# A sixth of the histogram's column masks moved from VectorE to ScalarE, and another order of the zeroing transfers among the weight loads

## The reference

```python
def _rgcn(x, edge_index, edge_type, weight, root, bias):
    src, dst = (edge_index[0], edge_index[1])
    msgs = x[src]
    out = x @ root + bias
    for r in range(weight.shape[0]):
        mask = (edge_type == r).astype(x.dtype)
        sums = jax.ops.segment_sum(msgs * mask[:, None], dst, num_segments=n)
        cnt = jax.ops.segment_sum(mask, dst, num_segments=n)
        mean = sums / jnp.maximum(cnt, 1.0)[:, None]
        out = out + mean @ weight[r]
    return out
```

## Time and profile before

| | |
|---|---|
| time, median of 3 runs | 1833.63 us (1831.04 to 1833.66) |
| the profiled execution's own time | 1833.66 us |
| its span, first to last instruction | 1832.0 us |
| PE busy | 1740.2 us, 95% |
| DVE busy | 996.4 us, 54% |
| ACT busy | 446.2 us, 24% |
| POOL busy | 712.9 us, 39% |
| mean granted clock of PE | 0.98 |
| queue q1 (SP's): share of 16 DMA engines | 23.5% |

### The profile page before, as it was taken

How to read it: one execution, slowest core, us unless ns; L and a number is a source line. 1 busy time by engine, 2 the same in 40 slices (tenths; PEclk the granted TensorE clock), 3 DMA queues, 4 the chain that set the end, 5 groups by cost and what they waited for, 6 DMA issues and landing times.

```text
span 1832.0 us, 27421 instructions
## 1 busy us (share of the span) xinstructions
PE 1740.2 (95%) x9548; PEld 1438.0 (78%) x9548; DVE 996.4 (54%) x2518; ACT 446.2 (24%) x848; POOL 712.9 (39%) x613
## 2 busy tenths in 40 slices
PE   5998999999999999999999999846999999999999
PEld 4775699978787777778787877634999888879987
DVE  6997999982625354443526286877612234351311
ACT  3327767730101011010101154433000000111100
POOL 2100010036363544536453554000785551446862
PEclk9999999999999999999999999957999999999999
DMA  4435432233231312122233532110454350113322
GB/s 131 132 121 162 127 109 94 88 120 95 61 91 36 95 35 85 46 74 61 65 85 121 175 115 85 29 47 7 130 179 140 104 157 26 47 46 127 89 73 68
DMA packets 132122, 168.42 MB, mean 92 GB/s; under 512 B 14383, under 2 KB 75963, under 8 KB 131767
## 3 DMA queue, kind: packets, MB, share of 16 engines
q1 hardware_dynamic: 104213, 128.21, 23.5%
q10 hardware_dynamic: 21730, 22.51, 3.8%
q0 software_dynamic: 6080, 16.40, 2.9%
HBM read 135.51 MB, written 25.30 MB: 88 GB/s over the span
## 4 chain that ended last, share of the span: by engine, by line
PE 80%; DVE 11%; DMA 3%; DVEq 2%; ACT 2%; issue 2%; POOL 1%; SPq 1%; ACTq 0%
PE ps L363 21%; PE ps L364 21%; PE ps L365 20%; PE ps L1383 9%; DMA w_stage<-in_stream 2%; PE ps L988 1%; DVE w_lo L314 1%; PE ps L1348 1%; DVE adj L974 1%; DVE key_start L868 1%; POOL w_lo L272 1%; PE ps L1303 1%; PE ps L922 1%; SPq L1038 1%; DMA nat<-in_x 1%
## 5 line engine op out<-in xcount | busy, mean ns | idle before, releaser
L363 PE MATMUL ps<-w_hi,xt_hi 128*125 128x512 f32 x1320 | 539.0, 408 | 12.6 <-DVE xt_lo L2260 3.5
L252 POOL TENSOR_TENSOR w_hi<-w_stage,zero 128x512 fp32r<-128x512 f32 x258 | 279.4, 1083 | 679.6 <-PE ps L365 654.7
L364 PE MATMUL ps<-w_lo,xt_hi 128*125 128x512 f32 x1320 | 523.1, 396 | 0.0
L365 PE MATMUL ps<-w_hi,xt_lo 128*125 128x512 f32 x1320 | 521.5, 395 | 0.0
L255 POOL TENSOR_TENSOR w_lo<-w_stage,w_hi 128x512 fp32r<-128x512 f32 x258 | 350.4, 1358 | 20.2
L363 PEld LDWEIGHTS ps<-w_hi,xt_hi 128*125 128x125 f32 x1320 | 246.5, 187 | 71.2 <-DVE xt_lo L552 4.4
L365 PEld LDWEIGHTS ps<-w_hi,xt_lo 128*125 128x125 f32 x1320 | 246.1, 186 | 63.3
L364 PEld LDWEIGHTS ps<-w_lo,xt_hi 128*125 128x125 f32 x1320 | 246.3, 187 | 53.3
L363 PE MATMUL ps<-xt_hi,w_hi 128*128 128x314 f32 x736 | 241.0, 327 | 0.8 <-DVE ring L2589 0.7
L365 PE MATMUL ps<-xt_hi,w_lo 128*128 128x314 f32 x736 | 226.0, 307 | 0.0
L364 PE MATMUL ps<-xt_lo,w_hi 128*128 128x314 f32 x736 | 225.8, 307 | 0.0
(11 more groups left out here) (431 smaller groups left out, 2163.7 us busy)
## 6 DMA issues: line engine op xcount, KB each, us to landing
w_stage<-in_stream SPq DMA_DIRECT2D x374, 256.0 KB, 2.7
pre<-ring POOLq DMA_DIRECT2D x30, 250.0 KB, 5.6
adj<-zeros SPq DMA_DIRECT2D x19, 321.8 KB
a_qt<-pre_t SPq DMA_DIRECT2D x18, 312.5 KB, 3.7
a_qt<-pre_t ACTq DMA_DIRECT2D x14, 312.5 KB
pre_t<-ring_t POOLq DMA_DIRECT2D x12, 312.5 KB, 2.8
pre_t<-ring_t ACTq DMA_DIRECT2D x12, 312.5 KB
a_vx<-pre SPq DMA_DIRECT2D x9, 312.5 KB
```

Source lines behind the costliest of these rows:

```text
L252: POOL.tensor_tensor(w_hi[:, q, :], w_stage[:, q % NST, :], zero[:].to_broadcast([128, 512]), ALU.add).then_inc(S("hi_done"), 1)
L363: PE.matmul(dst, l_hi, r_hi, start=first, stop=False)
L364: PE.matmul(dst, l_hi, r_lo, start=False, stop=False)
L365: return PE.matmul(dst, l_lo, r_hi, start=False, stop=last)
```

## The change

Three things change in the code.

- Column masks with c % 6 == 5, 40 of 240, are made by ACT in two operations (`hist_hot_act`): the distance |slot - key| into a new tile `col_off`, then relu(1 - distance) into `hot_col`. They have a semaphore of their own, `hi_act`, and PE waits for the one or the other. ACT makes mask c = 2g + 13 ahead of its copy of pair g.
- The addition waits for the one before it in DVE's queue instead of in the instruction, and DVE's order around it changes: the split comes ahead of the second addition, and where ACT makes the mask, the one mask left comes behind both additions.
- The zeroings stand in another place: five behind the load of chunk 39, then two behind each of the loads 40 to 46, none later.

```diff
+    col_off = [tmp(f"col_off{i}", [128, SPLIT], F16, 1) for i in range(2)]
...
-        DVE.drain()
+        return sig(DVE.drain(), "dve_step")
...
+    def hist_hot_act(c):
+
+        if c >= NHOT:
+            ALE.wait_ge(S("hi_pe"), c - NHOT + 1)
+        off = col_off[c // 6 % 2]
+        ALE.activation(off[:], col_key[:], ACT.Abs, scale=-1.0, bias=slot_col[:, c:c + 1]).then_inc(S("hi_act"), 1)
+        ALE.wait_ge(S("hi_act"), c // 6 * 2 + 1)
+        ALE.activation(hot_col[c % NHOT][:], off[:], ACT.Relu, scale=-1.0, bias=ones[:, 0:1]).then_inc(S("hi_act"), 1)
...
     def hist_add(c, start):
 
         DVE.wait_ge(S("hi_main"), c // 2 + 1)
+        if c:
+            DVE.wait_ge(S("hi_add"), c)
         o = adj[:, bass.ds(start, SPLIT)]
-        add = DVE.tensor_tensor(o, o, counts[c // 2 % 4][:, c % 2, :], ALU.add)
-        if c:
-            add.wait_op(S("hi_add"), c, "sem-ge")
-        add.then_inc(S("hi_add"), 1)
+        DVE.tensor_tensor(o, o, counts[c // 2 % 4][:, c % 2, :], ALU.add).then_inc(S("hi_add"), 1)
...
-            PE.wait_ge(S("hi_dve"), c + 1)
+            if c % 6 == 5:
+                PE.wait_ge(S("hi_act"), c // 6 * 2 + 2)
+            if c % 6 != 5:
+                PE.wait_ge(S("hi_dve"), c + 1 - (c + 1) // 6)
...
-        def zero_counts(i):
-            SP.dma_start(adj[:].bitcast(F32)[:, i * ZERO_RUN:(i + 1) * ZERO_RUN], zeros[:]).then_inc(S("ld_bt"), 16)
-
-        EARLY = ZERO // ZERO_RUN - 11
+        zeroed = 0
         for c in range(SC0 * KT, (SC0 + SC_GROUPS) * KT):
             load_chunk(c, c % NSL, (L0_ORDER[c // KT] - c // KT) * KT)
             if c == LAST_AHEAD:
                 wait(SP, mk_zeros)
                 wait(SP, mk_ranked)
-                for i in range(EARLY):
-                    zero_counts(i)
-            if c > LAST_AHEAD:
-                zero_counts(EARLY + c - LAST_AHEAD - 1)
+            for _ in range(0 if c < LAST_AHEAD else 5 if c == LAST_AHEAD else 2):
+                if zeroed < ZERO // ZERO_RUN:
+                    SP.dma_start(adj[:].bitcast(F32)[:, zeroed * ZERO_RUN:(zeroed + 1) * ZERO_RUN],
+                                 zeros[:]).then_inc(S("ld_bt"), 16)
+                    zeroed += 1
...
+        for c in range(5, LEAD_HOT, 6):
+            hist_hot_act(c)
         for h in range(HI_GROUPS):
             for n in range(per):
+                ahead = 2 * (h * per + n) + 1 + LEAD_HOT
+                if ahead % 6 == 5 and ahead < NCHUNK:
+                    hist_hot_act(ahead)
                 if chunk_at(h, n):
                     split_act(chunk_at(h, n))
                 hist_copy(h * per + n)
...
+                c = 2 * (h * per + n)
+                ahead = c + LEAD_HOT
+                by_act = ahead % 6 == 4
+                hist_add(c, starts[c])
+                if ahead % 4 == 0 and ahead < NCHUNK:
+                    hist_row(ahead)
+                if ahead < NCHUNK and not by_act:
+                    hist_hot(ahead)
+                if c % STARTS == 0 and c + STARTS < NCHUNK:
+                    starts.update(zip(range(c + STARTS, c + 2 * STARTS), hist_starts(c + STARTS)))
+                if chunk_at(h, n):
+                    split_dve(chunk_at(h, n))
+                hist_add(c + 1, starts[c + 1])
+                if ahead < NCHUNK:
+                    hist_hot(ahead if by_act else ahead + 1)
```

More of the change, by code:

```diff
@@ L1045, in beside @@
                 wait(SP, mk_ranked)
-                for i in range(EARLY):
-                    zero_counts(i)
-            if c > LAST_AHEAD:
-                zero_counts(EARLY + c - LAST_AHEAD - 1)
+            for _ in range(0 if c < LAST_AHEAD else 5 if c == LAST_AHEAD else 2):
[3 more added lines that the diff above has]
+                    zeroed += 1
+        assert zeroed == ZERO // ZERO_RUN
         for g in TURNED0:
@@ L1052, in beside @@
                 load_block(g * KT + s, s, L0_ORDER[g] * KT, s)
-                if g == TURNED0[0] and s < 3:
-                    zero_counts(EARLY + 8 + s)
         for c in range(C_REL, C_REL + AHEAD):
@@ L1102, in beside @@
         DVE.wait_ge(S("sc_pe"), sc_per + EC + 1)
-        slot_keys()
+        mk_slots = slot_keys()
         for c in range(4):
@@ L1111, in beside @@
                 hist_row(c)
-            hist_hot(c)
+            if c % 6 != 5:
+                hist_hot(c)
         HI0 = SC0 + SC_GROUPS
@@ L1150, in beside @@
         ALE.wait_ge(S("ld_bt"), 16 + 16 * (ZERO // ZERO_RUN))
+        wait(ALE, mk_slots)
+        for c in range(5, LEAD_HOT, 6):
+            hist_hot_act(c)
         for h in range(HI_GROUPS):
             for n in range(per):
+                ahead = 2 * (h * per + n) + 1 + LEAD_HOT
+                if ahead % 6 == 5 and ahead < NCHUNK:
+                    hist_hot_act(ahead)
                 if chunk_at(h, n):
```

## The result

The changed kernel takes 1848.83 us, median of 4 runs (1846.58 to 1850.19); the kernel before, beside it, 1832.96 us (1831.04 to 1833.66). The ratio is 1.0087, 95% interval 1.0069 to 1.0104: 15.9 us slower. The forecast was 1836.3 us with a range up to 1844, so the time lies outside it. Slower was the outcome with the largest chance in the prediction (0.44); the size was not foreseen.

What follows compares the result with a forecast made beforehand. PE, busy 1740.2 of 1832.0 us, was taken as the bound, with DVE (146.4) and PE (142.4) close in the histogram. 1833.66 + 2.2 (zeroings) + 0.4 (masks) + 0 (addition's wait) gave 1836.3 us, range 1830 to 1844.

Steps and rivals of the forecast that it cites:

- What bounds the kernel: Whole kernel: PE busy 1740.2 of 1832.0 us, so changes elsewhere count only where PE waits or its work shrinks.
- Two near bounds: Histogram: DVE at 146.4 us and PE at 142.4 both nearly bound the stage; ACT has some 38 us to spare.
- The zeroings, +2.2: Scatter: chunk 40's 6.2 us stall goes, but later chunks come late and the stretch ends 2.2 us later.
- second batch of stores: Scatter: later stores of `pre` sharing the DMA engines, taken to delay chunk 47 by 3.7 us, to 206.9.
- faster rival: Scatter: the chunk 40 stall goes and no wait returns, 1827.9 us; chance 0.14.
- second-batch rival: Scatter: the second batch of stores costs as much as the first, +10.4, 1844.5 us; chance 0.08.
- the 198.5: Scatter: time in us by which chunk 47 must land for the faster rival, said to be five steps after chunk 40.
- ACT's masks, +0.4: Histogram: moving a sixth of the column masks from DVE to ACT costs net 0.4 us.
- +5.0 and -4.6: Histogram: PE waits added by ACT's pairs (+5.0 us) against PE waits that DVE caused (-4.6 us).
- ACT's bunches: Histogram rival: Abs and Relu ahead of ACT's copies cost double, or DVE's waits stay: +5, 1840.9 us; chance 0.22.
- The addition's wait: Histogram: moving the wait into DVE's queue is hidden, 0.33 + 0.03 + 0.05 against 0.45 us, and costs 0.
- The upper bound: Histogram: if the moved wait were not hidden, the last additions would cost 12 x 0.05 = 0.6 us.

Runs made afterwards that it cites:

- experiment 8: Kernel before, with the wait on the last addition moved to DVE's queue for the even additions alone (119 of 240): 1846.72 us.
- experiment 3: Kernel before, with only the change's new order of the zeroings on SP's queue: 1835.88 us.
- The spread order: Kernel before, with five zeroings ahead of chunk 40 and then one behind each load: 1827.48 us and, again, 1828.67 us.

## Why the prediction was wrong

**What bounds the kernel: right.** The stage lengths show it. In every kernel in which no wait for the last addition lies uncovered the histogram takes 146.6 to 146.9 us (148.1 with the two waits swapped, which is covered but for 0.01 us a place), and PE waits 4.6 to 7.1 of it. "Two near bounds" was right too: as soon as DVE lost 0.08 us at every other addition, it was the bound (the stage took 158.4 us in experiment 8).

**The zeroings, +2.2: right.** Alone they cost 2.8 us. Single executions wait anything from 4.6 to 9.7 us with the old order and from 6.4 to 9.7 with the new one (experiment 3), so the mechanism and the size are borne out, and a match to a tenth is not. The late chunks 42, 43 and 44 were foreseen at 172.2, 178.5 and 184.7 and split at 170.57, 176.96 and 182.95, in an execution in which chunk 40 stood at 160.34 and not at 161.3. Chunk 46 came late as well (2.46 us), which was said to be in time, and chunk 47 stood at 206.31 for 206.9. The second batch of stores lies just there: POOL issues five from 187.33 on, and the DMA share is 0.86 between 188 and 192, where it is 0.45 from 184 to 188. That these stores made both late is argued from this; no run leaves them out. The loads land in the order of their issue: in the changed kernel those of chunks 40 to 47 (issued at 140.00 to 186.71) at 148.6, 162.9, 169.3, 175.5, 181.6, 187.8, 196.7 and 204.9. The prices of 2.57 us for a zeroing and 1.04 for a load carried over to that order: two zeroings and a load are 6.18, and chunks 42 to 45 land 6.4, 6.2, 6.1 and 6.2 us behind the one before. The spread order, which was planned on the same prices for 1826 to 1828 us, gave 1827.48 and 1828.67. The faster rival is out, the second-batch rival too. (In the faster rival, the 198.5 is right but lies six steps and the evacuation after chunk 40, not five.)

**ACT's masks, +0.4: right in the sum, in part by luck.** The stage grew by 0.3 us, but not by the two terms that gave 0.4. The pair takes 1.05 us and not 1.01, in the changed kernel's timeline:

```profile
283.62 0.55 ACT L961 ACTIVATE col_off<-col_key,slot_col 128x314 f16<-128x314 f16 x1
284.21 0.56 ACT L963 ACTIVATE hot_col<-col_off,ones 128x314 f16<-128x314 f16 x1
284.67 0.68 ACT L971 ACTIVATE counts<-ps 125x628 int16<-125x628 f32 x1
```

But ACT was busy 138.2 us of 146, not 143 to 150; PE's waits rose by 2.4 us in all, where the text had +5.0 and -4.6. PE's part of the stage became 1.5 us longer, and DVE's rest behind it 1.2 shorter, which the sum did not have. ACT's bunches as a rival (+5) did not come. The places with two additions side by side, 20 in the prediction, are 15 in the timeline, with four more that have a weight split between. The split is no part of the change: in the kernel before it stood ahead of the second addition as well. The view of the two lines has medians of 550 and 558 ns for the two operations, where I took the 520 of `ring_t`.

**The addition's wait: the step that failed.** The prediction said "0.33 + 0.03 + 0.05 against 0.45, so it is hidden", and for the places side by side "about 0.41", with bounds of 0 and 0.6 us. It measured 12.2 us on top of the masks and 15.0 alone. The sum had the end of an addition, the 0.03 us of the old wait and the duration of one register step. What runs is addition, semaphore step with the wait, register step, addition, and from end to start that takes 0.20 us and not 0.08. The sum is 0.33 + 0.20 = 0.53 against 0.45: not hidden, short by 0.08. Of the 0.20 the profile shows 21 + 46 = 67 ns as durations; the other 0.13 us are the three pauses of the chain shown above: 0.03 between the addition's end and the step that waited for it, and 0.05 behind each of the two steps. That 46 ns is how long the step executes, and it was read as how long the dependence takes through it.

With the distances of the changed kernel's timeline the stage adds up; this is an account made afterwards, not a forecast. It was 146.6 us and loses 8.4 with the masks. It gains 143 x (0.528 - 0.444) = 12.0 over single masks, 15 x (0.53 - 0.24) = 4.4 at the new places side by side, 9 x (0.53 - 0.39) = 1.2 at those that were so before, and 14 x (0.64 - 0.57) = 1.0 over a lone `hot_row` (0.57 is 0.24 for the addition and 0.33 for `hot_row`), and 0.5 over `hot_row` and a mask: 157.3 us. The stage took 157.9.

The upper bound failed for the same reason. "If they didn't, the last additions would cost 12 x 0.05 = 0.6" counted the last twelve additions and put the other 228 at nothing, on a margin of 0.45 - 0.41 = 0.04 us, which is less than one more queue step. In the kernel before 158 of them have nothing but a mask for cover, in the changed one 143, so each 0.05 us beyond the margin is about 7 us of DVE. Two steps more than the sum had would have been 0.51 against 0.45: 143 x 0.06 = 8.6 us, and 20 x (0.51 - 0.24) = 5.4 side by side, against the 8.4 that the masks free. That is 5.6 us, some 1842 in all, and still below 1848.8: not only the cover but the price itself, 0.20 and not 0.08 from end to start, had to be right.

The zeroings alone, the masks alone, and the wait on top of both sum to 2.8 - 0.35 + 12.2 = 14.6 us; the change measured 15.9. The 1.3 between lie inside the intervals (3 to 6 us wide), and nothing is made of them.

**Not settled.** The rows show where the 0.20 us go, and the swap that 0.07 of them go with the 21 ns step and its pause. What DVE's queue does in the three pauses is not shown by any run.

## What to carry to other kernels

Where an engine depends on its own last result, price that dependence from end to start in the trace, with every queue step behind the wait (here 0.13 us with one step and 0.20 with two), and keep the wait in the instruction (0.03), with the waits for long-done work ahead of it. A cover that is a tenth longer than what it covers (here 0.45 us against 0.41), over 240 places, is to be priced as if it were missed by a step or two. The backlog in SP's queue was removed by moving zeroings behind the point of need and spreading them one by one (5.3 and 6.0 us less); placed twice as densely right behind, they made the next loads late (2.8 us more).

## What the runs showed of the hardware that was not expected

- A dependent addition on DVE (125x314, int16) starts 0.03 us behind the end of the one that it waits for, if the wait is in the instruction. It is 0.13 with the wait at a register step of 46 ns ahead of it, and 0.20 with the wait at a semaphore step of 21 ns and the register step behind that.
- A further semaphore step on DVE's queue whose value had been reached cost nothing measurable, 238 times over (1833.37 us against 1833.48 in the same rounds).
- Abs and Relu of 128x314 with a pointer bias take 0.55 and 0.56 us on ACT, `ring_t` of the same size out of PSUM 0.52.
